# Between the two layers: the second half's chunks gated one at a time, and dense expert passes moved later

## The reference, cut to what matters

```python
xn = layernorm(x)
s = attention0(xn)                    # 16 heads of 8, softmax, relative bias
g = silu(ffn0(xn))                    # 8 experts, 2 chosen, shared part, layernorm with gamma, beta
x = x + s * g
xn = layernorm(x)
s = attention1(xn)                    # attention over channels: q and k normalised over the tokens
g = silu(ffn1(xn))                    # 4 experts, hidden 512
x = x + s * g

def ffn1(x):                          # per token
    logits = gelu(x @ rW1 + rb1) @ rW2 + rb2
    p = softmax(logits); the 2 largest p are the weights of their experts
    return sum over the 2 chosen e of p[e] * (gelu(x @ We1[e] + be1[e]) @ We2[e] + be2[e])
```

## Time and profile before

| | before |
|---|---|
| median of 3 runs | 818.03 us |
| the profiled execution | 818.58 us, span of its profile 816.7 us |
| TensorE (PE) busy | 692.3 us, 85% |
| weight loads (PEld) | 485.4 us, 59% |
| VectorE (DVE) | 550.4 us, 67% |
| ScalarE (ACT) | 485.2 us, 59% |
| GpSimd (POOL) | 450.8 us, 55% |
| mean granted TensorE clock | 0.942 |

### The profile page before, as it was taken

One profiled execution on the slowest core, in us unless ns is written; L12 is line 12 of the kernel. 1 busy time (PEld: TensorE's weight loads), 2 busy tenths in 40 slices (PEclk: granted clock), 3 DMA queues, 4 the chain that ended last, 5 costly groups with the idle time before them and its releaser, 6 DMA issues. The chain is left out here.

```text
span 816.7 us, 17080 instructions
## 1 busy us (share of the span) xinstructions
PE 692.3 (85%) x5313; PEld 485.4 (59%) x5313; DVE 550.4 (67%) x1291; ACT 485.2 (59%) x934; POOL 450.8 (55%) x397
## 2 busy tenths in 40 slices
PE   3967888999999999799999898998956477999890
PEld 2741332333333333389998787898856376988790
DVE  6999999999999998333333678357357474454346
ACT  4864676888888888554455375786612244534351
POOL 6933447889889899834554444100055652454442
PEclk9998999999999999799999999999888579999995
DMA  7973532323233321468887865500012310778875
GB/s 232 278 235 115 171 106 72 88 85 91 73 96 83 91 76 56 131 195 243 266 254 245 280 202 165 174 2 1 2 39 92 117 49 24 212 225 243 248 231 164
DMA packets 96461, 117.44 MB, mean 144 GB/s; under 512 B 10552, under 2 KB 72296, under 8 KB 96408
## 3 DMA queue, kind: packets, MB, share of 16 engines
q1 hardware_dynamic: 88376, 100.22, 41.4%
q0 software_dynamic: 8032, 16.58, 5.9%
HBM read 82.30 MB, written 34.32 MB: 143 GB/s over the span
## 5 line engine op out<-in xcount | busy, mean ns | idle before, releaser
L803 POOL DMA_INDIRECT yg_dram<-work x135 | 133.5, 989 | 157.1 <-DVE work L2015 93.4
L1422 ACT ACTIVATE work<-wide,work 128x256 f32<-128x256 f32 (+1 forms) x324 | 129.5, 469 | 124.9 <-PE wide L1045 115.3
L1580 DVE TENSOR_REDUCE work<-wide 128x4 bf16<-128x1024 f32 x128 | 153.8, 1225 | 9.2 <-PE wide L906 5.3
L1056 PE MATMUL wide<-work 128*128 128x128 f32 x1272 | 156.6, 277 | 0.0
L1056 PEld LDWEIGHTS wide<-work 128*128 128x128 f32 x1272 | 150.7, 194 | 0.9
L1045 PE MATMUL wide<-xT,work 128*128 128x256 f32 (+1 forms) x552 | 131.2, 381 | 11.5 <-issue 8.5
L1045 PEld LDWEIGHTS wide<-xT,work 128*128 128x128 f32 x552 | 99.1, 192 | 25.2 <-issue 13.7
L765 POOL TENSOR_TENSOR work<-work,biasT 128x1024 f32<-128x1024 f32 x32 | 75.8, 2370 | 38.3 <-ACT work L1360 37.8
L2012 DVE TENSOR_TENSOR work<-wide,work 128x256 f32<-128x256 f32 x69 | 28.9, 419 | 87.9 <-PE wide L1056 63.9
L765 POOL TENSOR_TENSOR yy<-yy,biasT 128x1024 f32<-128x1024 f32 x32 | 75.6, 2363 | 22.1 <-ACT yy L1360 21.2
L906 PE MATMUL wide<-biasA,turnb 128*128 128x512 bf16 x256 | 79.4, 392 | 0.0
(11 more groups left out here) (318 smaller groups left out, 1144.1 us busy)
## 6 DMA issues: line engine op xcount, KB each, us to landing
work<-in_wcat SPq DMA_DIRECT2D x73, 578.0 KB
xg_dram<-empty SPq DMA_DIRECT2D x35, 260.0 KB, 2.7
work<-xg_dram SPq DMA_DIRECT2D x66, 130.0 KB
stk_dram<-yy SPq DMA_DIRECT2D x16, 384.0 KB, 3.7
...
```

What stands on the lines that cost most here:

```text
L803: g.indirect_dma_start(out=yg_dram[l], out_offset=bass.IndirectOffsetOnAxis(ap=yid[v][:, s_:s_ + 1].bitcast(u32), axis=0), in_=yb[v][:, s_ ...
L1056: last = mm(YP[u][:, s_ * D:(s_ + 1) * D], hb[u][:, c, s_ * P:(s_ + 1) * P], wb[v][:, HID + c * D:HID + (c + 1) * D], start=(c == 0), stop ...
L1422: A(hb[u][:, c, 0:n * P], bank[2 + 2 * u + c // 2][:, (c % 2) * TS:(c % 2) * TS + n * P], ACT.Gelu, bias=wb[v][:, bc:bc + 1]).then_inc(m[" ...
L1580: V.tensor_reduce(nmax[:, :, 2 * place(t):2 * place(t) + 2].rearrange("p c e -> p e c"), into[:, :].rearrange("p (e c k) -> p e c k", e=2, ...
```

## The change

Three things change, and the rest follows from banks and counts.

1. The second half's two chunks are finished, gated and normalised one at a time: `finish_half(1, ...)` becomes `finish_chunk(2, ...)` and `finish_chunk(3, ...)`, and batches 8 to 11 and 12 to 15 go through the router as two pipelines, each behind its own chunk. The first half's router takes one turn after each of the passes 0 to 5 and two turns without a pass.
2. Passes 6, 7 and 8 stand beside the routing, where 10 and 11 stood; the turning of the weights goes ahead of them, into bank 0, and its copy ahead of `route_act`.
3. Passes 9, 10 and 11 run inside the Gram loop: `up_rows` in turns 1, 5, 9, `gelus` in turns 3, 7, 11, `down_rows` in turns 4, 8, 12, `keep_dense` in turns 6, 10, 14. For their banks the Gram products use bank 0 alone, the weights' products bank 1 and banks 2 and 3.

```diff
-TURN = {0: 0, 1: 1, 2: 2, 3: 3, 5: 4, 6: 5, 7: 6, 8: 7}
-NDA = NDJ - 2
+NDA, NDB = NDJ - 6, NDJ - 3
+LATE_UP, LATE_GELU, LATE_KEPT = ({at + 4 * i: NDB + i for i in range(NDJ - NDB)} for at in (1, 3, 6))
+LATE_DOWN = {at + 3: j for at, j in LATE_UP.items()}
...
# TensorE
-            for j in range(NDA):
+            for j in range(NB // 2):
                 v = j % NWB
...
+                if j < NDA:
...
+                    up_rows(m, j, v, xTd[j // E1])
+                pe.wait_ge(pre[1]["xT"], min(j + 2, NB // 2 - 1) + 3)
+                if j:
+                    router_logits(j - 1, (j - 1) % 2)
+                router_hidden(j, j % 2)
                 if j == 1:
                     pe.wait_ge(moe[0]["y"], NJ0 + 4)
-                if j:
+                if 0 < j <= NDA:
                     down_rows(m, j - 1, (j - 1) % NWB)
...
+            router_logits(NB // 2 - 1, 1)
             pe.wait_ge(m["gelu"], NDA * 4 + 8)
-            pe.wait_ge(pre[1]["lg"], 2 + 1)
-            staged([(transpose_normalised, 1), (router_hidden, 2), (router_logits, 3)], NB // 2, NB)
+            for lo in (NB // 2, NB * 3 // 4):
+                staged([(transpose_normalised, 1), (router_hidden, 2), (router_logits, 3)], lo, lo + NB // 4)
...
             pe.wait_ge(pre[1]["lg"], 2 + 2)
-            for j in (NDA, NDA + 1):
-                up_rows(m, j, j % NWB, xTd[j // E1])
-            down_rows(m, NDA, NDA % NWB)
             for k in range(2):
-                last = tr(bank[2][:, k * D:(k + 1) * D], wqk1_sb[:, k * D:(k + 1) * D], ident[:, :])
+                last = tr(bank[0][:, k * D:(k + 1) * D], wqk1_sb[:, k * D:(k + 1) * D], ident[:, :])
             last.then_inc(A1["WT"], 1)
+            dense_up(NDA)
+            dense_up(NDA + 1)
+            dense_down(NDA)
             route_pe(1, E1, bank[0], bank[1])
-            down_rows(m, NDA + 1, (NDA + 1) % NWB)
+            dense_up(NDA + 2)
+            dense_down(NDA + 1)
+            dense_down(NDA + 2)
             pe.wait_ge(rou[1]["kept"], 1)
...
                 pe.wait_ge(a["x2"], b + 1)
-                pe.wait_ge(a["Cs"], b + 1)
+                pe.wait_ge(a["Cs"], b + 2)
...
                 pe.wait_ge(a["Cs"], b + 3)
-                pe.wait_ge(a["uu"], b + 1)
-                mm(bank[2 + u][:, 0:D], cc[u], wqk1_sb[:, 0:D], start=True, stop=True)
+                pe.wait_ge(a["uu"], b + 2)
+                mm(bank[1][:, 0:D], cc[u], wqk1_sb[:, 0:D], start=True, stop=True)
...
+            def late_pass(b, u, turn):
+                if b in LATE_DOWN:
+                    dense_down(LATE_DOWN[b])
+                if b in LATE_UP:
+                    pe.wait_ge(m["y"], NDB + 4)
+                    dense_up(LATE_UP[b])
+
-            staged([(gram, 1), (gram_times_weights, 2)])
+            staged([(gram, 1), (gram_times_weights, 2), (late_pass, 0)])
# ScalarE
-                act.wait_ge(com[0]["x1"], b // (NB // 2) + 1)
+                act.wait_ge(com[0]["x1"], b // 4 if b >= NB // 2 else 1)
...
-                if j in (4, 5):
-                    normalise_gate(j - 2)
-                elif j == 6:
+            for j in range(NB // 2):
+                if j < NDA:
+                    gelus(moe[1], j, j % NWB, 16)
+                hidden(j, j % 2)
+                if j + 3 < NB // 2:
+                    transposed_again(j + 3, (j + 3) % 2)
+                if j + 4 < NB // 2:
+                    normalised(j + 4)
+                if j == 3:
+                    normalise_gate(2)
+                elif j == 4:
+                    normalise_gate(3)
                     silu(0, 2)
                     silu(0, 3)
...
+            act.wait_ge(A1["WT"], 1)
+            A(wqkT, bank[0][:, 0:2 * D], ACT.Copy)
             route_act(1, E1)
...
+            staged([(copy_gram, 1), (copy_product_rows, 2), (late_gelus, 0)])
# VectorE
             keep_dense(0)
+            finish_chunk(2, com[0]["stats"])
             add_choices(0, 3)
             add_shared(3)
+            keep_dense(1)
             gate_stats(3)
-            keep_dense(1)
-            finish_half(1, com[0]["stats"])
...
+            finish_chunk(3, com[0]["stats"])
+            keep_dense(2)
             gamma_beta(2)
+            keep_dense(3)
+            gamma_beta(3)
+            add_gated(2)
+            row_stats(2)
+            finish_chunk(2, com[0]["x1"])
+            keep_dense(4)
+            add_gated(3)
+            row_stats(3)
             keep_dense(5)
...
+            finish_chunk(3, com[0]["x1"])
             router_logits(0)
```

99 lines of the change are left out of this document (40 added, 59 removed).

## The result

The changed kernel takes 827.94 us (median of 15 runs, 819.67 to 831.53) where the kernel before takes 817.55 beside it: ratio 1.0105, interval 1.008 to 1.013. All ratios leave out executions more than 1.5% above the fastest of the same kernel, six of twelve in `one_pipe`, four of twelve in `chunks_only` and at most three elsewhere, and the profiled ones of `down8_free` and `half_look` are among those left out. The profiled execution took 831.53 us, its span is 829.8 us and its mean granted clock 0.924, against 818.58, 816.7 and 0.942.

A forecast was written before the change was run, and what follows sets the result against it. The end of the second layer's attention was taken to set the kernel's end. Logits 6.0 us early, last slot 5.7, products 2.8, all given back in the Gram loop: 818.0 us, own range 815 to 821, outer 810 to 826.

The forecast's parts named there:

- rival 2: TensorE at half clock in the second chunk's router, some 3.5 us, making the kernel slower: 823.7 us; chance 0.23.
- R: Point where the second half's router logits are complete; forecast 576.5 us, 6.0 early.
- The hole: TensorE waiting for batch 5's gelu, late in ScalarE's queue: 6.8 us from 542.8.
- G: Point where ScalarE begins to normalise batch 8; forecast to move from 564.2 to 557.7, bounds 555.7 and 560.1.
- F: Reference point added with the results, not forecast: VectorE's first instruction on the second half's fetched rows.
- G to R: From batch 8's normalising to complete logits, in two pipelines: 8.7 us for four batches, 18.75 for both, 0.5 more.
- R to S: From complete logits to last slot: exponent 1.6 us later, most hidden, 0.3 stays.
- S: Point where the routing's last slot is known; forecast 5.7 us early.
- R to the products: From complete logits to the Gram loop's first products: 18.3 us instead of 15.06, cost 3.2.
- The Gram loop: Late passes 9 to 11 there cost 3.0 us behind the scatters' window; single banks cost nothing.
- rival 1: Late passes are absorbed in the Gram loop's disturbed window and queues, so 5.7 us stays won: 812.3 us; chance 0.27.
- The similarity loop: Second loop of the second layer's attention: keeps its length, some 49 us.

The follow-up runs named there:

- one_pipe: The changed kernel with the second half's eight batches as one router pipeline, chunks still finished one by one; ratio 1.0045 to the kernel before.
- chunks_only: The kernel before with only the second half finished chunk by chunk, in one router pipeline; ratio 1.0053 to the kernel before.
- down8_free: The changed kernel with pass 8's `down_rows` no longer waiting for VectorE's `keep_dense(6)`; ratio 1.0039 to the kernel before.
- half_look: The changed kernel with the second half finished as one, one router pipeline and ScalarE's silus later; ratio 1.0157, the kernel before taking about 782 us.
- at 817: Occasions on which the unchanged kernel before takes 816.6 to 819.0 us (medians).
- fill_look: The changed kernel with 14 extra matmuls in TensorE's hole, second run; ratio 1.0077, the kernel before taking about 782 us.
- before_look: The kernel before, unchanged, profiled a second time beside itself; ratio 1.0001, the kernel before taking about 817 us.
- pipe_down8: The changed kernel with silus one turn later, one router pipeline and pass 8's `down_rows` freed of its `keep_dense(6)` wait; ratio 0.9954 to the kernel before.
- At 782: Occasions on which the unchanged kernel before takes 781.5 to 782.0 us (medians).
- act_pipe: The changed kernel with silus one turn later and one router pipeline; ratio 1.0066, the kernel before taking about 782 us.

## Why the prediction was wrong

The measured 827.9 lies 10 us over the forecast of 818.0, 7 over its own range (815 to 821) and 2 over the outer one (810 to 826). Of the rivals, rival 2 (the clock) names the mechanism that was most at work up to R, at 823.7, and the comparison at 1.0050 has a median of 823.5. That nearness is luck: the rival put the half clock in the second chunk alone, and 5.2 of its 5.7 us rest on a dearer Gram loop that wasn't measured at 817.

- **The hole.** Forecast 6.8 us from 542.8, with ScalarE's queue as its cause; measured 7.46 (7.04 and 6.58 in the other profiles), same cause and place. Right.
- **G.** Forecast 557.7, bounds 555.7 and 560.1; measured 560.32, or 559.1 with the 1.2 us ahead of F taken off. From the first matmul behind the hole to G I took 8.1 us, 2.0 of it for the clock; measured 9.4, with the first three groups all at half clock (7.2 us for 4.0) and the next two at full. fill_look, at full clock, takes 6.3. So the term was 1.3 us too small.
- **G to R, the step that failed most.** Forecast 18.75 us, measured 23.2, 21.3, 21.3. I took 8.7 us for a chunk at full clock. At full clock it is right (8.7 us in fill_look), but each chunk began at half clock (windows 562 to 568 and 574 to 580: 0.53, 0.72). I gave this a rival of its own, for the second chunk only, "about 3.5 us"; it is 2.5 to 4.5 for both. The evidence against that I quoted, eight batches of before at full clock, was of a single full pipeline, and one_pipe shows that such a pipeline runs at full clock behind its start (1.00 from 568 on, 0.87 in 562 to 568). So R was not 6 us early but 1.1 late, 0.2 early counted from F.
- **R to S.** Exponent 1.54 us later (forecast 1.6), S 0.34 later (forecast 0.3). The number is right by luck, and the reason is weaker than I thought: the cover of 1.80 us in the earlier trace rows was there because the up passes of the earlier trace rows ran at half clock. In before_look they ran at full clock, R to S is 12.9, and the copy ahead of the exponent then costs 1.8 us. I took one execution's slack for the kernel's.
- **R to the products.** Forecast 18.3 us, measured 21.8. The term of 3.2 us became 6.7; from S alone it was 3.9, and pipe_down8, without the wait, has 4.2. I let pass 8's second down pass start right behind pass 7's; it waits for VectorE's `keep_dense(6)`, which is queued behind the slots. The prediction named `keep_dense(8)` and missed this other wait of the same semaphore. It is 1.98 us in the trace and 2.0 in down8_free; another 1.2 is the late release of the first product.
- **The Gram loop.** Forecast +2.8 us, measured -0.3 (36.1 against 36.4). This looks like rival 1, but its mechanism holds for the pair 4, 5 alone: turns 8, 9 and 12 cost 3.3 us in after, near my figure, and shorter late releases pay them back. At 782 the loop is 5.9 us longer, twice my figure, and 0.9 of it are the single banks, which I put at nothing.
- **The similarity loop** kept its length (51.8 against 51.2). Right.
- **The start of the experts** was 4.2 us slower in the profiled execution, by a clock that varies from execution to execution; no step of mine had that.

My sum was -6.5 + 0.5 + 3.2 + 2.8 = 0.0 against F; measured is -5.1 + 5.0 + 6.7 - 0.3 = 6.3. Three terms were too small, by 1.4, 4.5 and 3.5 us, and one too large by 3.1. The last two cancel but for 0.4 us, and that is luck too: from S to the end of the Gram loop I had 5.7 us more than before, and 6.1 were measured. So nearly the whole miss, 5.9 of 6.3 us, was made up to R: I priced the half clock at 2.0 us behind the hole and at nothing in the two pipelines.

What stays open: what makes a release late; why TensorE's clock falls behind the entry's wait in one_pipe and act_pipe and not in after; and why the experts start at half clock in some executions and not in others.
